# A graph network's last layer: one joined weight matrix for the messages, and the degree term added on VectorE

## What is computed

```python
def _L3_gnn_ref(x, edge_index, W_in, b_in, W_msg, W_ih, b_ih, W_hh, b_hh, W_out, b_out):
    src, dst = (edge_index[0], edge_index[1])
    h = x @ W_in.T + b_in
    m = h @ W_msg
    agg = jax.ops.segment_sum(m[src], dst, num_segments=n_nodes)
    gi = agg @ W_ih.T + b_ih
    gh = h @ W_hh.T + b_hh
    i_r, i_z, i_n = jnp.split(gi, 3, axis=-1)
    h_r, h_z, h_n = jnp.split(gh, 3, axis=-1)
    r = jax.nn.sigmoid(i_r + h_r)
    z = jax.nn.sigmoid(i_z + h_z)
    n = jnp.tanh(i_n + r * h_n)
    h_new = (1.0 - z) * n + z * h
    return h_new @ W_out.T + b_out
```

## Time and profile before

| what | us |
|---|---|
| median of 3 runs | 2643.17 (2642.38 to 2643.97) |
| the profiled execution, its own time | 2647.27 |
| its span | 2645.6 |
| PE busy in it | 2351.0 (89%) |
| DVE busy | 1587.1 (60%) |
| ACT busy | 1185.7 (45%) |
| last sum over edges taken by DVE (L1498), which starts the last layer | 2479.05 |
| last step's rows added by DVE (L1653) | 2641.07 |

### The profile page before, as it was taken

One profiled execution on the slowest core, in us unless ns is written; L12 is line 12 of the kernel. 1 busy time (PEld: TensorE's weight loads), 2 busy tenths in 40 slices (PEclk: granted clock), 3 DMA queues, 4 the chain that ended last, 5 costly groups with the idle time before them and its releaser, 6 DMA issues.

```text
span 2645.6 us, 58999 instructions
## 1 busy us (share of the span) xinstructions
PE 2351.0 (89%) x20705; PEld 2077.7 (79%) x20705; DVE 1587.1 (60%) x2721; ACT 1185.7 (45%) x3044; POOL 109.5 (4%) x88
## 2 busy tenths in 40 slices
PE   1479999999999999999987799999998625999897
PEld 1369999999999999999965577777787614888654
DVE  8667777777777777777845455555575483000033
ACT  1235555555555555555511466666786410000133
POOL 3100000000000000000000000000000240000000
PEclk6579999999999999999955899999999857999899
DMA  6401111111111111111133522223384146888222
GB/s 165 124 33 74 73 73 58 63 73 73 73 51 70 73 73 73 49 73 73 73 91 91 173 106 105 105 105 105 143 313 162 47 118 255 309 301 301 91 62 56
DMA packets 183684, 299.35 MB, mean 113 GB/s; under 512 B 13256, under 2 KB 136523, under 8 KB 183523
## 3 DMA queue, kind: packets, MB, share of 16 engines
q1 hardware_dynamic: 179488, 284.33, 31.2%
q0 software_dynamic: 4144, 14.34, 2.0%
HBM read 198.15 MB, written 100.49 MB: 113 GB/s over the span
## 4 chain that ended last, share of the span: by engine, by line
PE 80%; DVE 9%; DMA 3%; DVEq 3%; issue 3%; ACT 1%; POOLq 0%; POOL 0%; SPq 0%; ACTq 0%; PEldq 0%
PE ps L703 20%; PE ps L762 18%; PE ps L692 15%; PE ps L686 8%; PE ps L746 7%; PE ps L801 5%; PE ps L895 2%; PE ps L732 2%; DVE hT_s L1272 1%; DVE carry L1469 1%; DVE big L1198 1%; DMA hs<-node_rows 1%; PE ps L792 1%; PE ps L620 1%; DMA big<-edge_counts 1%
## 5 line engine op out<-in xcount | busy, mean ns | idle before, releaser
L1001 ACT CAST edge_area<-ps 128x392 f16<-128x392 f32 x784 | 385.8, 492 | 504.9 <-PE ps L686 504.8
L703 PE MATMUL ps<-big,rows_area 128*128 128x128 f32 x4802 | 571.3, 276 | 0.0
L762 PE MATMUL ps<-big,rows_area 128*128 128x256 f16 (+1 forms) x4900 | 542.7, 271 | 25.3 <-DMA big<-edge_counts 25.3
L703 PEld LDWEIGHTS ps<-big,rows_area 128*128 128x128 f32 x4802 | 550.8, 192 | 0.0
L692 PE MATMUL ps<-edge_area 128*128 128x196 f16 x4704 | 542.1, 250 | 0.0
L762 PEld LDWEIGHTS ps<-big,rows_area 128*128 128x128 f16 x4900 | 469.0, 98 | 78.2 <-DMA big<-edge_counts 25.6
L692 PEld LDWEIGHTS ps<-edge_area 128*128 128x128 f16 x4704 | 422.5, 97 | 0.4
L1007 ACT COPY big<-ps 128x392 f32<-128x392 f32 x784 | 383.9, 490 | 10.4 <-PE ps L692 1.8
L686 PE MATMUL ps<-edge_area 128*128 128x196 f16 x2352 | 334.7, 250 | 14.6 <-DVEq L1421 14.6
L1416 DVE TENSOR_TENSOR edge_area<-lo_pair,carry 128x768 f16<-128x768 f16 x392 | 218.8, 558 | 202.4 <-PE ps L692 125.2
L1417 DVE TENSOR_TENSOR edge_area<-cell_pair,carry 128x1176 f16<-128x1176 f16 x392 | 299.4, 764 | 0.0
(11 more groups left out here) (210 smaller groups left out, 1665.7 us busy)
## 6 DMA issues: line engine op xcount, KB each, us to landing
big<-edge_counts SPq DMA_DIRECT2D x336, 448.0 KB, 5.0
edge_counts<-edge_area SPq DMA_DIRECT2D x49, 1568.0 KB, 5.7
hs<-node_rows POOLq DMA_DIRECT2D x21, 448.0 KB, 4.5
edge_area<-in_x SPq DMA_DIRECT2D x14, 448.0 KB, 4.5
x_stream<-edge_area SPq DMA_DIRECT2D x14, 448.0 KB, 4.1
node_rows<-edge_area SPq DMA_DIRECT2D x14, 448.0 KB, 3.0
edge_area<-x_stream SPq DMA_DIRECT2D x14, 448.0 KB, 3.8
node_rows<-rows_area SPq DMA_DIRECT2D x7, 448.0 KB, 3.0
```

The source lines that it names most:

```text
L703: last = mm(p_sum[par], h0[:, n, :], w32[:, par, n, :], start=(n == 0), stop=(n == NB - 1))
L762: last = mm(p_block[par][:, 0:width, :], planes[:, p, sh, :], piece[:, par, k, 0:width, j, :], start=(sh == 0 and p == 0), stop=(sh == NB ...
L1001: nc.scalar.copy(store_slot[:, par, :, cols], p_count[s % 2]).then_inc(sem("count_taken"), 1)
```

## The change

Ahead of the third layer's loop PE turns `WinT` around (a product with the identity), and behind it multiplies it with `Wmsg` to `msg_of_sum` (128 by 128), and `Wmsg` with `b_in` to `msg_of_one` (128 by 1); ACT copies each out of PSUM. In the last layer PE forms the messages in one product of `msg_of_sum` with `agg` into `pC`; the product with `WinT`, the one-row product with the degrees, `messages(i)` and ACT's two copies L1148 and L1150 are gone. DVE instead has `take_messages(i)`: degrees times `msg_of_one` plus `pC`, written to `am_s`. The degrees come spread over 128 partitions, one step of 896 at a time, in two slots of `carry`, each step by one transfer on SP's queue. DVE's loop is written out for its last step. Many semaphores that nobody waits for get one common name, `passed`, without another effect on the order.

```diff
-        deg_row = rows_area.view(0, NPAD)
+        deg_s = carry.view(0, 2 * W)
...
-        am_s, ah_s, t_s, newT_s = (edge_area.view(n * W, W) for n in range(4))
+        am_s, t_s, newT_s = (edge_area.view(n * W, W) for n in range(3))
+        win_rows = edge_area.view(EDGE_WORDS - D, D)
...
+        msg_of_sum = sb("msg_of_sum", [P, D])
+        msg_of_one = sb("msg_of_one", [P, 1])
...
@@ def _(sp):
+            def load_degrees(i):
+                sp.dma_start(steps_of(deg_s, i % 2), deg_dram[:, bass.ds(i * W, W)].to_broadcast([P, W])).then_inc(
+                    sem("deg_row_in"), 16)
+
+            load_degrees(0)
+
             sp.dma_start(hs[:], rows_of(rows_dram, 0)).then_inc(sem("h_in4"), 16)
             sp.dma_start(xs2[:, 0:W].rearrange("p (b d) -> p b d", d=D), rows_of(x_dram, 0)).then_inc(sem("x_in4"), 16)
-            sp.wait_ge(sem("agg_done3"), 1)
-            sp.dma_start(deg_row[0:1, :], deg_dram[:, 0:NPAD]).then_inc(sem("deg_row_in"), 16)
...
             with sp.Fori(0, NS - 1) as i:
 
+                sp.wait_ge(sem("msg_sum_s"), i + 1)
+                load_degrees(i + 1)
                 sp.wait_ge(sem("hT4"), i + 1)
                 sp.dma_start(hs[:], rows_of(rows_dram, i + 1)).then_inc(sem("h_in4"), 16)
...
@@ def _(pe):
             mm(pA[:, 0:D], last_clique[:], wt["WcT"][:], start=True, stop=True).then_inc(sem("clique_lin"), 1)
+            mm(pD[:, 0:D], wt["WinT"][:], ident[:], start=True, stop=True).then_inc(sem("win_flipped"), 1)
...
+            pe.wait_ge(sem("win_rows"), 1)
+            mm(pD[:, TILE:TILE + D], win_rows, wt["Wmsg"][:], start=True, stop=True)
+            mm(pD[:, TILE + D:TILE + D + 1], wt["Wmsg"][:], b_in[:], start=True, stop=True).then_inc(sem("weights_joined"), 1)
             pe.wait_ge(sem("x_new"), 2 * NS)
             branch(pe, order, sum_any(3), multiply(3))
...
                 pe.wait_ge(sem("n_in"), i + 1)
-                wide(pC, [(wt["WinT"][:], step_view(agg, i)),
-                          (bias["b_in_row"][:], step_view(deg_row, i, slice(0, 1)))]).then_inc(sem("hid_sum"), 1)
-
-            def messages(i):
-
-                pe.wait_ge(sem("hid_sum_s"), i + 1)
-                wide(pD, [(wt["Wmsg"][:], fixed_view(ah_s))]).then_inc(sem("msg_sum"), 1)
+                wide(pC, [(msg_of_sum[:], step_view(agg, i))]).then_inc(sem("msg_sum"), 1)
...
             pe.wait_ge(sem("agg_done3"), 1)
-            pe.wait_ge(sem("deg_row_in"), 16)
+            pe.wait_ge(sem("sum_weights"), 2)
             for name in ("r_ready", "z_ready", "n_in", "y_ready"):
                 pe.sem_inc(sem(name), 1)
             hidden(0)
-            messages(0)
             with pe.Fori(0, NS - 1) as i:
                 gates(i)
                 hidden(i + 1)
                 output(i)
-                messages(i + 1)
...
@@ def _(act):
+            act.wait_ge(sem("win_flipped"), 1)
+            nc.scalar.copy(win_rows, pD[:, 0:D]).then_inc(sem("win_rows"), 1)
...
+            act.wait_ge(sem("weights_joined"), 1)
+            nc.scalar.copy(msg_of_sum[:], pD[:, TILE:TILE + D]).then_inc(sem("sum_weights"), 1)
+            nc.scalar.copy(msg_of_one[:], pD[:, TILE + D:TILE + D + 1]).then_inc(sem("sum_weights"), 1)
             act.wait_ge(sem("agg_done3"), 1)
...
-                act.wait_ge(sem("hid_sum"), i + 1)
-                nc.scalar.copy(ah_s, pC[:, 0:W]).then_inc(sem("hid_sum_s"), 1)
-                act.wait_ge(sem("msg_sum"), i + 1)
-                nc.scalar.copy(am_s, pD[:, 0:W]).then_inc(sem("msg_sum_s"), 1)
...
@@ def _(dve):
-            with dve.Fori(0, NS) as i:
+
+            def take_messages(i):
+                dve.wait_ge(sem("deg_row_in"), i * 16 + 16)
+                dve.sem_inc(sem("passed"), 1)
+                dve.wait_ge(sem("msg_sum"), i + 1)
+                V.scalar_tensor_tensor(out=am_s, in0=steps_of(deg_s, i % 2), scalar=msg_of_one[:, 0:1], in1=pC[:, 0:W],
+                                       op0=ALU.mult, op1=ALU.add).then_inc(sem("msg_sum_s"), 1)
+
+            dve.wait_ge(sem("sum_weights"), 2)
+            take_messages(0)
+
+            def gru(i, more):
                 dve.wait_ge(sem("n_gate"), i + 1)
                 dve.wait_ge(sem("r_ready"), i + 2)
                 V.scalar_tensor_tensor(out=t_s, in0=pD[:, 0:W], scalar=b_hn, in1=r_s, op0=ALU.add, op1=ALU.mult)
                 dve.drain()
                 V.tensor_tensor(t_s, t_s, pC[:, 0:W], ALU.add).then_inc(sem("n_in"), 1)
+                if more:
+                    take_messages(i + 1)
                 dve.wait_ge(sem("tanh"), i + 1)
...
+            with dve.Fori(0, NS - 1) as i:
+                gru(i, True)
+            gru(NS - 1, False)
```

More of the change, by code:

```diff
@@ L338, in step @@
                     sp.wait_ge(sem("x_seen"), i + 1 + s * NS)
-                    sp.sem_inc(sem("sp_passed"), 1)
+                    sp.sem_inc(sem("passed"), 1)
                     sp.wait_ge(sem("rows_out"), i * 16 + 16 + s * NS * 16)
                     if new_x:
-                        sp.sem_inc(sem("sp_passed"), 1)
+                        sp.sem_inc(sem("passed"), 1)
                         sp.wait_ge(sem("x_out"), i * 16 + 16 + (s - 1) * NS * 16)
@@ L542, in f @@
                         pool.wait_ge(sem("g_mm"), j * (2 * NT) + mm_base(l) + 2 * NT)
-                        pool.sem_inc(sem("g_slots_taken"), 1)
+                        pool.sem_inc(sem("passed"), 1)
                         nc.gpsimd.tensor_copy(chunk_slot[:], index[:, bass.ds(j * 2, 2)])
@@ L553, in idle @@
             def idle():
-                pool.sem_inc(sem("idle"), 1)
+                pool.sem_inc(sem("passed"), 1)
             def load_rows(name, used):
@@ L560, in load_rows @@
                     pool.wait_ge(sem(used), i + 1)
-                    pool.sem_inc(sem("rows_used"), 1)
+                    pool.sem_inc(sem("passed"), 1)
                     pool.dma_start(hs[:], rows_of(rows_dram, i + 1)).then_inc(sem(name), 16)
@@ L579, in normalise @@
                 pool.wait_ge(sem("x_new"), i + NS)
-                pool.sem_inc(sem("norm_begun"), 1)
+                pool.sem_inc(sem("passed"), 1)
                 nc.gpsimd.tensor_tensor(norm, f_all[:, bass.ds(i * SB, SB), :], over_rows(gain), ALU.mult)
@@ L699, in weigh @@
                     pe.wait_ge(sem("weight_taken"), h * SGS + SGS + 4)
-                    pe.sem_inc(sem("pe_passed"), 1)
+                    pe.sem_inc(sem("passed"), 1)
                     pe.wait_ge(sem("sum_taken"), h + 1)
@@ L896, in wide, with step_view @@
                 return last
-            def step_view(v, i, rows=slice(0, P)):
-                return lambda lo, n: v[rows, bass.ds(i * W + lo, n)]
+            def step_view(v, i):
+                return lambda lo, n: v[:, bass.ds(i * W + lo, n)]
             def fixed_view(v):
@@ L997, in take_supergroup @@
                     act.wait_ge(sem(f"half_saved{par}"), i * 16 + 16)
-                    act.sem_inc(sem("act_passed"), 1)
+                    act.sem_inc(sem("passed"), 1)
                 act.wait_ge(sem("count_ready"), h * SGS + s + 1)
@@ L1035, in idle @@
             def idle():
-                act.sem_inc(sem("idle"), 1)
+                act.sem_inc(sem("passed"), 1)
             def count_pieces():
@@ L1488, in take_block @@
                         dve.wait_ge(sem(f"deg_in{par}"), i * 16 + 16)
-                        dve.sem_inc(sem("dve_passed"), 1)
+                        dve.sem_inc(sem("passed"), 1)
                     n = width * SUBD
```

1 line of the change is left out of this document (added).

## The result

The changed kernel takes 2653.43 us (median of 6 runs, 2649.81 to 2656.04), the kernel before 2642.78 (6 runs); the ratio is 1.0039, 95% interval 1.0026 to 1.0052. The forecast was 2652.5, in a range of 2645 to 2664, and "slower by over 0.2%" with a chance of 0.79. The change is slower by some 10 us (by the interval, 7 to 14).

The account below looks back on a forecast made before the run. The last layer's output was taken as bound by a tie of PE's and DVE's strands. +9.8 (steps) + 9.0 (clock) - 9.5 (start) = +9.3 us, giving 2652.5 against the median of 2643.17, range 2645 to 2664.

Parts of the forecast that it names:

- Part 1: Last layer's rounds: DVE's new operation and its wait for PE add 2.58 us per round, +9.8 over six against today's.
- Part 2: Clock in the last layer's rounds: PE's 4.8 us gap puts every output at the low clock, +1.5 each, +9.0 us.
- rival B: Low clock goes on into the last layer's gates, +15 to +18 us: 2658 to 2666; chance 0.24.
- Part 3: Start of the last layer: no degree-row transfer to wait for, fewer products and copies; 5.5 to 12.7 us gained, -9.5 taken.
- Part 4: Joining the weights, loading spread degrees and renaming semaphores cost nothing; hs lands after 6 to 7 us, still in time.
- rival C: Degrees or hs land late, transposes wait 1 to 2 us per round, +6 to +12: about 2661; chance 0.07.
- Rival D: Faster: start gains 12.7 us and the joined product is ready before tanh, rounds under 21.7; chance 0.04.

Follow-up runs that it names:

- e2: Changed kernel plus five unread 128 by 512 products on PE per step from the second on, behind the msg_of_sum product: 2643.1 us, ratio 0.9999 to the kernel before.
- e4: Changed kernel with joined weights, but the degree term as a one-row PE product and an ACT copy instead of DVE's operation: 2635.3 us, ratio 0.9975 to before.
- e1: Changed kernel with DVE's take_messages moved behind the operation that forms the new hidden rows: 2633.7 us, ratio 0.9954 to the kernel before.
- e6: Changed kernel with PE's msg_of_sum product ahead of the WinT product instead of behind it: 2651.7 us, ratio 1.0037 to the kernel before.
- e10: Changed kernel with DVE's take_messages operation done a second time, into an unread tile, in each step but the last: 2669.6 us, ratio 1.0098 to the kernel before.
- e5: Changed kernel with the output in pD instead of pA and PE's y_ready wait only ahead of the n gate's product: 2647.6 us, ratio 1.0026 to before.
- e7: Changed kernel with take_messages behind the new hidden rows, output in pD and the later y_ready wait: 2620.0 us, ratio 0.9926 to the kernel before.
- e8: e7 plus two unread 128 by 512 products on PE per step from the second on: 2616.3 us, ratio 0.9911 to the kernel before.
- e3: Kernel before with its degree row kept in carry and loaded ahead of the last layer, nothing else of the change: 2639.2 us, ratio 0.9983 to the kernel before.
- e9: e8 with the load of hs issued ahead of the spread degrees on SP's queue: 2617.4 us, ratio 0.9906 to the kernel before.

## Why the prediction was right, and where its steps were off

**Part 1, the steps: right.** The operation came out at 1.15 and L1664 starts 2.93 after the product with msg_of_sum starts (2571.63 - 2568.70), for which 3.03 was forecast (2617.03 - 2614.00). The output follows DVE in every round, and the gates follow the reading of its rows. The round at full clock was put at 22.2 and is 22.4 (e2). What is missing is the way from L1672's end to the gates: I took 0.05 us and it is 0.29 (2579.62 to 2579.91), 1.4 over six rounds. That joining alone leaves the rounds as they are (e4) and that the place alone is worth over 18 (e1; at full clock 22.42 against 19.84 in each round, which is 15.5 over the six, and the rest is the clock) shows the cause that was named.

**Part 2, the clock: right in kind, short in size.** The forecast was 1.5 per round, the low clock in every output, and the gates fast again. Five rounds did just that, 23.5 to 23.9. In one the first gate product was low too (25.16 in all). The term of 9.0 came out at 143.9 less 134.3 (e2) = 9.6. What the sum did not see is how near rival B was: with the output 0.7 us earlier and the products in another order (e6), or 1.05 later (e10), it is the usual case, and with no wait ahead of the gates (e5) too. Its chance of 0.24 was not too high.

By the Trainium skill (TensorE: Matmul & The Clock Gate, section "HAM oscillation — how this bites in real kernels"), PE's wait in each iteration brings the low clock in each; the trace of the changed kernel agrees, six of six outputs at 2.95 to 3.29. The trace of e1 does not: PE waits 2.16 ahead of each output, and three of six are at 1.83. So the rule held here for the longer wait, and the measurements decide for the shorter one.

**Part 3, the start: mis-sized.** -9.5 was taken from a span of 5.5 to 12.7; it was 12.6. The step that failed is the guess that PE would start at the low clock and rise on the way. With the transfer gone PE's gap is 1.13, and the clock did not fall in this trace: the transposes took 0.96 and WinT 1.77. A row for this was there: the gap of 0.99 ahead of WinT does not end in a low clock. But e1 has the same start and WinT at 3.28, 1.5 more, so the 12.6 is the better end of what this start gives.

**The sum.** +20.8 in the rounds for +18.8, -12.6 at the start for -9.5, and -0.4 behind: +7.8 in the layer for +9.3. The two errors go against each other, and the median rose by 10.6 where the traces give 7.8; that 2652.5 lies only 0.9 from 2653.4 is luck in part. **Part 4** held: `hs` landed after 6.1 us, as put (6 to 7), and no step of the changed kernel waited for it. How little was left is shown by e5, e7 and e8, where PE did wait for it (0.27 to 0.93): taking away the gates' wait for y_ready was enough, in one step of e5, to make rival C's mechanism real. Rival D's condition was built (e6): the product is then ready 0.7 earlier, not before tanh, and nothing is won.

## What to carry to other kernels

An operation moved from a busy engine to an idle one costs by its place in the idle engine's queue: with a wait inside a strand that everything follows, a 1.15 us operation, done six times, cost 18 to 20 us, and three operations further on, in the shadow of the other engine's work, nothing (19.8 a round at full clock with it, e1, and without it, e4). Work that is removed may have been a cover; look for what it hid (here the reading of the output rows), and give that reading a buffer of its own before the cover goes. Where TensorE waits in each round, reckon with the low clock on top of the wait, and ask how far it reaches.

## What was not expected of the hardware

The price of a gap on PE is not smooth. Gaps ahead of the output of 2.16 us let the clock fall in three of six rounds (e1), of 4.74 in all; at 5.79 (e10), but also at 3.23 with the products in another order (e6), it was still low for the first gate products in four of six rounds. With the gates following at once (e5, 4.74) it was low for them behind five of six outputs. In the kernel before the clock fell in three of six rounds with no gap over 1 us, where one-row products stand between the full ones. So it did in e3, and in e4, which keep them (e4 also has the wait of 1.53 ahead of the gates); in e2, e8 and e9, with full products in that place, it fell in no round but one of e8, in which PE had waited for `hs`. Whether one-row products do less for the clock than full ones was not tried by itself and stays open. They are not the whole of it: in the start of e1 the clock fell behind gaps of 1.13 and 1.08 with none of them near.

Two DVE operations without a drain between them start 1.06 apart though each takes 1.15 (2548.45 and 2549.51 in e10). And 448 KB spread from one row of memory to 128 partitions landed after 4.9 us, hardly more than 448 KB of rows, but made the transfer queued behind it 2 us later (6.1 instead of 4.1, and 4.2 in e9, where that transfer goes first).
